# Two rows of sums side by side in DRAM, and five input reloads placed ahead of the late rows, in a recurrent layer with a mixture of experts

## The reference

```python
xn = _layernorm(x, axis=-1)
s = _L0_attn_ref(xn, ...)          # projections, a gate, a linear recurrence of 8 states over the sequence
g = _silu(_L0_ffn_ref(xn, ...))    # router + 32 experts + one shared expert
return x + s * g

# inside _L0_ffn_ref: N = 8192 tokens, E = 32 experts, K = 4 per token, cap = 1280 rows per expert
w, idx = _gate(xf, wg)
xe = xp[buf_tok].reshape(E, cap, DIM)
h = silu(xe @ w1) * (xe @ w3)                 # per expert, 256 x 256
out = (h @ w2) * buf_w
y = zeros(N + 1, DIM).at[buf_tok].add(out)[:N]
z = silu(xf @ sw1) * (xf @ sw3) @ sw2         # shared expert
return y + z
```

## Time and profile before

| what | value |
|---|---|
| median of 3 runs | 1086.96 us (1084.85 to 1091.03) |
| the profiled execution | 1084.01 us |
| its span (first to last instruction) | 1082.2 us |
| PE busy | 993.8 us (92%) |
| DVE, ACT, POOL busy | 782.9, 589.8, 720.8 us |
| moved by DMA | 195.57 MB, mean 181 GB/s |

### The profile page before, as it was taken

How to read it: one execution, slowest core, us unless ns; L and a number is a source line. 1 busy time by engine, 2 the same in 40 slices (tenths; PEclk the granted TensorE clock), 3 DMA queues, 4 the chain that set the end, 5 groups by cost and what they waited for, 6 DMA issues and landing times.

```text
span 1082.2 us, 29821 instructions
## 1 busy us (share of the span) xinstructions
PE 993.8 (92%) x8059; PEld 949.1 (88%) x8059; DVE 782.9 (72%) x2542; ACT 589.8 (54%) x1129; POOL 720.8 (67%) x560
## 2 busy tenths in 40 slices
PE   5678898988888899999999999999999999999984
PEld 4668887887877899999999999999999999999931
DVE  6677888887777676677667776776777777777774
ACT  4668888888886344444444444444444444444453
POOL 1067777777777775767888766666666766676640
PEclk8799999999999999999999999999999999999998
DMA  9943443334444887978898887789778888987699
GB/s 274 303 164 128 143 143 140 137 134 145 145 143 147 257 202 150 201 144 174 167 182 156 165 195 155 147 196 203 159 164 195 172 192 182 194 195 146 142 299 348
DMA packets 174867, 195.57 MB, mean 181 GB/s; under 512 B 19865, under 2 KB 166594, under 8 KB 174786
## 3 DMA queue, kind: packets, MB, share of 16 engines
q1 hardware_dynamic: 120848, 123.15, 38.8%
q0 software_dynamic: 53312, 71.50, 34.2%
q10 hardware_dynamic: 626, 0.01, 0.0%
HBM read 92.15 MB, written 106.09 MB: 183 GB/s over the span
## 4 chain that ended last, share of the span: by engine, by line
PE 66%; POOL 9%; issue 7%; DVE 5%; ACT 5%; DMA 4%; SPq 2%; DVEq 0%; POOLq 0%; ACTq 0%
PE h L922 13%; PE h L924 13%; PE h L923 13%; POOL slot_rows L794 8%; PE yb L942 7%; PE yb L940 7%; PE yb L941 6%; PE xt L906 6%; DMA y_sum<-y_more,y_idx 1%; DMA slot_rows<-rows 1%; ACT rows L1182 1%; DVE act L1507 1%; SPq L472 1%; DVE raw L1516 1%; DMA x_all<-L_attn_x 1%
## 5 line engine op out<-in xcount | busy, mean ns | idle before, releaser
L922 PE MATMUL h<-xh,w_hl 128*128 (+1 forms) x1392 | 410.0, 295 | 4.3 <-DVE xl L1501 3.0
L924 PE MATMUL h<-xl,w_hl 128*128 (+1 forms) x1392 | 394.4, 283 | 0.0
L923 PE MATMUL h<-xh,w_hl 128*128 (+1 forms) x1392 | 393.0, 282 | 0.0
L759 POOL DMA_INDIRECT y_sum<-x_all,dest_top x168 | 267.4, 1592 | 109.7 <-DVE x_all L1778 62.1
L794 POOL DMA_INDIRECT slot_rows<-rows,dest_idx x256 | 261.0, 1020 | 110.8 <-issue 69.5
L1255 ACT ACTIVATE acth<-act 128x512 fp32r<-128x512 f32 x174 | 109.7, 631 | 316.9 <-PE yb L942 294.1
L922 PEld LDWEIGHTS h<-xh,w_hl 128*128 128x128 f32 x1392 | 264.4, 190 | 6.9 <-issue 5.8
L923 PEld LDWEIGHTS h<-xh,w_hl 128*128 128x128 f32 x1392 | 264.8, 190 | 0.0
L924 PEld LDWEIGHTS h<-xl,w_hl 128*128 128x128 f32 x1392 | 264.4, 190 | 0.0
L1511 DVE TENSOR_TENSOR actl<-act,acth 128x512 fp32r<-128x512 f32 x174 | 120.4, 692 | 181.5 <-ACT acth L1255 181.3
L940 PE MATMUL yb<-w_hl,acth 128*128 128x256 f32 x696 | 196.7, 283 | 3.9 <-DVE y_more L1778 2.7
(11 more groups left out here) (236 smaller groups left out, 1443.1 us busy)
## 6 DMA issues: line engine op xcount, KB each, us to landing
rows<-slot_rows SPq DMA_DIRECT2D x127, 289.0 KB, 3.5
raw<-L_ffn_w SPq DMA_DIRECT2D x99, 256.0 KB, 2.7
slot_rows<-rows SPq DMA_DIRECT2D x48, 289.0 KB, 9.4
x_all<-L_attn_x SPq DMA_DIRECT2D x16, 512.0 KB, 6.7
out<-s_all SPq DMA_DIRECT2D x32, 256.0 KB, 5.2
y_sum<-yw SPq DMA_DIRECT2D x31, 256.0 KB
x_all<-L_attn_x SPq DMA_DIRECT2D x20, 256.0 KB
x_all<-slot_rows SPq DMA_DIRECT2D x15, 289.0 KB, 3.8
```

The source lines that it names most:

```text
L759: pool.indirect_dma_start(y_dram, bass.IndirectOffsetOnAxis(y_index(buf, t), 0), y_out[buf][:, t, :], None, bounds_check=token_bound, oob_ ...
L922: mm(out, high, xh[:, k, cols], start=(k == 0), stop=False)
L923: mm(out, low, xh[:, k, cols], start=False, stop=False)
L924: ins = mm(out, high, xl[:, k, cols], start=False, stop=(k == KD - 1))
```

## The change

Two edits, which do not depend on one another.

First, the rows of `y_dram` within a pair are put in another order. Before, row t x 128 + p of a pair's 256 rows belonged to partition p and tile t; now it is row 2 x p + t, so that the two rows of 1 KB that a partition writes (z) or reads (y) lie side by side in DRAM, 2 KB in one piece. The token numbers that the additions use as indices follow (`token`), and so the additions go to the new places. The stores of the output and the loads of x keep the old order.

Second, SP waits for `set_free` and issues the five reloads of x before it issues the loads of the late pairs' rows, not after them.

```diff
@@ store_z, and the same in the store of the last pair (L596) and in load_y (L686)
-                sp.dma_start(y_dram[bass.ds(q * PAIR, PAIR), :].rearrange("(t p) c -> p t c", p=P),
+                sp.dma_start(y_dram[bass.ds(q * PAIR, PAIR), :].rearrange("(p t) c -> p t c", p=P),
                              yw[:, :, :]).then_inc(z_stored, 16)
@@ SP, after the section of expert 31
             for n in range(3):
                 load_raw(E + 1, n, 1)
+            sp.wait_ge(set_free, 1)
+            for c in range(SET):
+                load_x_again(c)
             fifth = is_fifth(0)
             with sp.If(fifth > 0):
                 load_rows(0, PAIRS, 0)
...
             pairs_all = sp.snap(taken)
-            sp.wait_ge(set_free, 1)
-            for c in range(SET):
-                load_x_again(c)
@@ POOL, setup
-            pool.iota(token[:, :], [[P, TILES]], 0, 1, allow_small_or_imprecise_dtypes=True).then_inc(consts_ready, 1)
+            pool.iota(token[:, :], [[PAIR, A_PAIRS], [1, 2]], 0, 2, allow_small_or_imprecise_dtypes=True).then_inc(consts_ready, 1)
```

More of the change, by code:

```diff
@@ L595, in _ @@
             sp.wait_ge(z_ready, 2 * A_PAIRS)
-            sp.dma_start(y_dram[(A_PAIRS - 1) * PAIR:, :].rearrange("(t p) c -> p t c", p=P),
+            sp.dma_start(y_dram[(A_PAIRS - 1) * PAIR:, :].rearrange("(p t) c -> p t c", p=P),
                          last_z[:, :, :]).then_inc(last_z_stored, 16)
@@ L680, in _ @@
             pairs_all = sp.snap(taken)
-            sp.wait_ge(set_free, 1)
-            for c in range(SET):
-                load_x_again(c)
             def load_y(c):
-                sp.dma_start(y_buf(c), y_dram[tail_tokens(c), :].rearrange("(t p) c -> p t c", p=P)
+                sp.dma_start(y_buf(c), y_dram[tail_tokens(c), :].rearrange("(p t) c -> p t c", p=P)
                              ).then_inc(y_loaded[c], 16)
```

## The result

| | before | changed |
|---|---|---|
| median | 1086.76 us (6 runs, 1084.85 to 1091.03) | 1098.03 us (6 runs, 1096.02 to 1100.29) |
| ratio | | 1.0106, 95% interval 1.0091 to 1.0121 |
| the profiled execution, its span | 1084.01, 1082.2 us | 1096.02, 1094.2 us |

What follows compares the result with a forecast made beforehand. PE bounds the experts; the end is PE, additions and transfers in series without slack. Stop 10.0 + clock 1.3 - contention 0.3 - rows 0.4 = +10.6 us on 1086.96, some 1097.5 us; range 1091 to 1102.

Steps and rivals of the forecast that it cites:

- The end is three links in series without slack: Kernel's end: PE up to (31,4)'s product, then additions, then transfers; a delay of that product delays the end.
- `set_free` stays where it is, and the late rows are queued behind it: SP's queue: reloads still start at 1018.28 us; rows of (1,3) are issued after them, at 1022.84.
- PE's stop, +10.0 us: PE ahead of (1,3)'s transposes: waits from 1016.21 until the rows land at 1026.2; range +8.0 to +12.0 us.
- The clock, +1.3 us: PE behind the stop: 12 matmuls and four transposes run at granted clock 0.50; 0 to +2.4 us.
- Less contention for (31,4)'s additions, -0.3 us: POOL's additions of (31,4): no reload in flight beside them, so they land sooner; 0 to -1 us.
- DVE has nothing else to do meanwhile: During PE's stop: ACT and DVE have no other work, so they hide none of it.
- The order of rows, -0.4 us: The 32 loads of y: 2 KB pieces are about 3% cheaper per byte than 1 KB; 0 at worst.
- B: Loads of y: time goes with number of pieces, so they cost half; -12 against +11, about 1087 us; chance 0.07.
- C: Additions beside loads of y: they wait longer behind 2 KB packets, +2.4 us, 1100 us median; chance 0.16.
- D: PE's stop and after: half the stop is given back, +4 to +7 us, about 1092.5 us; chance 0.15.

Runs made afterwards that it cites:

- The kernels that keep PE busy: Changed kernel plus 84 matmuls with unread results ahead of the wait for (1,3)'s rows; ratios to before 1.0095, 1.0092 and 1.0097 in three comparisons.
- the last kernel above: Changed kernel with set_free raised early, inside expert 31's section, and the reloads back behind the late rows; 1084.64 us, ratio 0.9996 to before.
- the first two experiments: Each one edit alone against the kernel before: the order on SP, 1098.62 us, ratio 1.0115; the order of rows, 1083.97 us, ratio 0.9989.

## Why the prediction was right

It said 1097.5 us (1091 to 1102), and 1098.03 was measured. The mechanism is the one forecast; that the two numbers lie within 0.6 us is in part luck, since errors of its terms cancelled, and since the change cost 11.5, 11.0 and 13.3 us in three comparisons, against 10.6 forecast. Its steps:

- **The end is three links in series without slack.** Right. The first load of y is 12.5 us later than before (12.7, 12.3, 12.6, reckoned from (0,3)), and from it to the end the changed kernel takes 51.8, 54.1 and 52.8 us, before 53.4. The delay goes through whole.
- **`set_free` stays where it is, and the late rows are queued behind it.** Right: reloads from 1019.23, which is 6.78 us behind the transposes of (0,3); before, 6.78 us as well.
- **PE's stop, +10.0 us.** Measured 10.3 to 11.1. Two errors in its working nearly cancelled. The five reloads are issued in 2.5 us, not the 3.42 of the earlier trace rows, and the rows land in 4.5 to 5.6 us, not in the 3.4 of the earlier trace rows. The extra landing behind the reloads, which I had put in the range with "up to 1.5 us", should have stood in the sum, and was 2.2 us in one trace.
- **The clock, +1.3 us.** Under-sized. The mechanism is as forecast, but the low level reached into the down projection of (31,4): through all 12 of its matmuls in the first trace of the changed kernel, through four of them in the other two. The cost is 2.2 us up to the first load of y. I had taken its length from a single fall; here PE ran at 0.21 us a matmul for 6.0 us behind the start in the first trace and for 4.3 in the other two.
- **Less contention for (31,4)'s additions, -0.3 us.** Its landing took 3.69 us instead of 3.85. The kernels that keep PE busy need 12.2 us from the transposes of (1,3) to the first load of y, before 12.6: 0.4 us in all. A part of it, 0.2 us, is not contention: DVE scales the product 5.0 us behind the transposes in the first of these kernels, before 5.2, since its splits of the next weights (1.28 us) fall into the stop. So "DVE has nothing else to do meanwhile" was wrong by that much.
- **The order of rows, -0.4 us.** Measured -1.2, with an interval from -2.5 to 0; -0.4 lies inside, and a gain isn't shown beyond doubt, since the last kernel above, with the same edit, is 0.4 us faster than before (1.5 faster to 0.8 slower). The estimate that time goes with bytes is borne out: a load of y got some 8% cheaper to issue and the last stage 0.8 us shorter at most, not half as long.

The sum of the parts as measured is 10.7 + 2.2 - 0.4 - 1.2 = 11.3 us, which is what the two edits apart give (12.5 - 1.2) and what was measured (11.5, and 11.0 and 13.3 in the repeats). The terms are uncertain by a microsecond or so each, so that they agree to a tenth is chance. By them the prediction's 10.6 was low by less than a microsecond, with the clock too small by 0.9 and the stop by 0.7, against a gain from the rows that was too small by 0.8.

Of the rivals, B and C are out by the first two experiments; D, a stop half given back, is out by the table, since none of the stages behind takes it up. By the Trainium skill, "Perfetto Trace Analysis", section "DMA Optimizations", the pieces of 2 KB could have brought much; the runs show 0 to 2.5 us of 1085. For C, the prediction took the packet of the Trainium skill, "DMA: Bandwidth & Descriptors", section "Queues, rings and completion order", to be one piece of 1 or 2 KB; there it is a group of several such pieces, so the page doesn't describe C's turns piece by piece.

## What to carry to other kernels

A queue engine runs its stream in order, so a wait put ahead of a load is a wait for that load's user: before moving a transfer forward, look when its condition comes true and what stands behind it. Here a condition that came true at 1018.3 was put ahead of rows that PE wanted at 1016.2. A stop of the matrix engine can be dearer than its length: here the clock fell with it, and stops of 10 to 11 us cost 2.2 us more. And if a wait has to go forward, the signal that ends it can often be raised earlier, which took back 8 of the 11 us here.

## What was not expected of the hardware

- Behind a stop of 2.0 us the granted clock still fell to 0.50, and it fell only after PE had started again at 1020.09 (1.00 in 1020.0 to 1020.5, 0.78 in 1020.5 to 1021.0, 0.50 in 1021 to 1024, with PE busy throughout). The time at the low level after stops of 10 to 11 us differed between executions of one program: the step back came 6.0 us behind the start in one and 4.3 us in two.
- A load of 289 KB that landed in 3.4 us by itself took 4.5 to 5.6 us with five loads of 256 KB issued ahead of it on the same queue.
- Landings of (31,4)'s additions took little longer beside five reloads (3.85 and 4.35 us) than with none (3.6 to 3.7 us in ten traces).
- Between executions of the same program the point just ahead of the change, after a millisecond, moves by up to 2.5 us (2.9 over all twelve traces); the difference of two spans alone would have mis-sized each part of 1 to 2 us here.
